# DLRM tower with a two-layer CIN: TensorE spreads the first chunk's layer-1 operands with zero-one matrices, and the order of gathers and products moves

## The chip, the cores and the metric

The kernel runs on one core of a Trainium2 chip. Its time is the device time of one execution in microseconds; the number for a kernel is the median of its runs. One further execution is recorded by the hardware profiler, and all rows below come from that one.

## The reference, cut to what matters

512 samples have 32 ids each. Each id picks a row of 32 floats from its table, so a sample becomes `e[32 fields, 32 dims]`. A compressed interaction network with two layers follows, then a small dense network.

```python
e = stack([tbl_f[ids[:, f]] for f in range(32)], axis=1)        # 512 x 32 x 32
prev = e
for W in (filter_0, filter_1):                                  # 1024 x 128, 4096 x 128
    z = einsum('bhd,bmd->bhmd', e, prev)                        # h: 32 fields, m: 32, then 128
    prev = relu(einsum('bpd,pn->bnd', z.reshape(b, h * m, d), W))
    outs.append(prev)
z = sum(concatenate(outs, axis=1), axis=-1)                     # 512 x 256
h = relu(concatenate([z, dense_ctx]) @ W_top1 + b_top1)
h = relu(h @ W_top2 + b_top2)
y = h @ W_top3
```

## The kernel before

**Chunks and tiles.** The 512 samples go through in 32 chunks (`CHUNKS`) of four tiles. A tile is four samples times 32 dims, 128 columns, one sample from each quarter of the batch; a chunk has 512 columns (`COLS`). Buffers are double, by the parity `p` of the chunk. The last chunks, and the first two, are written out; those between run in a hardware loop of two chunks an iteration (`over_chunks`).

**Layer 1.** Products of two fields of one sample are needed for all pairs. The kernel holds the fields on partitions four times (`x_same`: field f on partitions 4f to 4f+3) and a shifted copy (`x_shift`: for group g and shift s, field f + 4s + g). DVE multiplies the two into `z` (`products`, L482): `which` 0 is groups 0 and 1, 1 is groups 2 and 3, and 2 is the last shift of 16 fields from `x_pair` into `z_last`. PE multiplies `z` by the folded weights `v` into the bank `acc1` (`layer1`, L671): four fp32 matmuls and one of the last shift, whose operand is split into two rounded parts by ACT (`round_last`, L375) and POOL (`lower_last`, L256).

**How the operands get on the partitions.** POOL gathers the rows of a chunk by four indirect DMAs, one a tile (`gather`, L249), into `emb`. SP writes `emb` twice into the DRAM tensor `x_rows`, waits, and reads it back in the spread form with six DMAs (`chunk` of SP, L192): `x_same`, `x_shift` groups 0 and 1, `x_pair` three times, `x_shift` groups 2 and 3. SP starts on chunk c when layer 1 of chunk c - 2 is done and the four gathers of c have landed.

**Layer 2.** ACT (`relu1`, L362) and DVE (`lower`, L501) split layer 1's result into a high and a low part. For each tile PE makes eight banks of 512 (`layer2`, L690), three matmuls a bank. Even banks (`t_act`, a ring of two) are weighted by ACT (`weigh_tile`, L390), odd banks (`t_dve`, a ring of four) by DVE (`add_tile`, L520), which adds onto ACT's results in `prod`. POOL then folds `prod`: `halve` (L264) adds one half onto the other with an accumulating DMA, and `fold` (L279), called one tile later, adds the rest into `side`. `relu2` of ACT and `lower2` of DVE round the result, and PE sums it over the dims (`pooling`, L714) at the end of the next chunk. DVE's `lower2` of chunk c - 1 stands ahead of its tile 3 of chunk c.

**Order.** Each engine has its instructions in a fixed order, written by hand; semaphores tie the engines. In chunk c, DVE does: transpose of c+1 (the weights for layer 2), tile 0, products 0 of c+2, tile 1, products 2 of c+2, tile 2, `lower` and `pooling1` of c+1, `place`, `lower2` of c-1, tile 3, products 1 of c+2. PE does tile 0, layer 1 of c+1 (two matmuls), tile 1, layer 1 of c+1 (the rest), tiles 2 and 3, pooling. POOL, tile by tile: `halve` of the tile, gathers for chunk c+3, `fold` of the tile before. Behind `halve` of tile 0 it issues one gather, behind tile 1 one, behind tile 2 two.

**Start.** ACT loads layer 2's weights in eight pieces, six of them first and two once chunk 0's `x_rest` has landed; ACT rounds them (`upper_w`), DVE takes the remainder (`lower_w`). PE runs 14 dummy matmuls (`warm_up`) once `x_rows` of chunk 0 is written, then layer 1 of chunk 0 (`first_layer1`, L658), eight dummy matmuls, then the chunks. Products 0, 2 and 1 of chunk 1 stand before DVE's chunk 0. POOL gathers chunks 0 to 2, waits for ACT's rounding of chunk 1's last shift and does `lower_last(1, 1)` before its chunk 0.

Of the kernel before, what the change touches and what calls it, by code (L numbers as in the profile page):

```python
# [28 lines left out]
W_PIECES = BANKS  # L29
W_EARLY = 6  # L30
W_PIECE = FIELDS * MAPS // W_PIECES
# [7 lines left out]

def dlrm_tower(nc, table, ids, dense, w0a, w0b, w0c, w1, wt1, bt1, wt2, bt2, wt3, select, identity, out):  # L40
    fp32, f32r, i32 = mybir.dt.float32, mybir.dt.float32r, mybir.dt.int32
# [4 lines left out]
    with ExitStack() as ctx:  # L46
# [33 lines left out]
        cur2_hi = [sb(f"cur2_hi{p}", [128, TILES, MAPS], f32r) for p in range(2)]  # L80
        cur2_lo = [sb(f"cur2_lo{p}", [128, TILES, MAPS], f32r) for p in range(2)]
        sel_wide = sb("sel_wide", [128, SEL_WIDE])
        sel = [sb(f"sel{p}", [128, 128], f32r) for p in range(2)]
# [44 lines left out]
        x_rest = [sem(f"x_rest{p}") for p in range(2)]  # L128
        out_written = sem("out_written")
        ids_ready = sem("ids_ready")  # L130
        row_ids_ready = sem("row_ids_ready")
# [52 lines left out]
        def before(c, parity):  # L184

            return (c - parity) // 2

        @block.sync
        def _(sp):
            sp.dma_start(raw_ids[:, :], ids).then_inc(ids_loaded, 16)  # L190

            def chunk(c, p):  # L192
                turn = before(c, p) + 1

                wait(sp, layer1_done, c - 1)
# [8 lines left out]
                first, stride = src.offset, COLS  # L204

                def shifted(first_group, groups):

                    return bass.AP(src.tensor, first + first_group * stride,
                                   [[stride, FIELDS], [GROUPS * stride, SHIFTS], [1, groups * COLS]])

                sp.dma_start(x_same[p][:, :],
                             bass.AP(src.tensor, first, [[stride, FIELDS], [0, SHIFTS], [1, COLS]])).then_inc(x_first[p], 16)
                sp.dma_start(x_shift[p][:, 0:WHOLE, :].rearrange("p g c -> p (g c)"),
                             shifted(0, WHOLE)).then_inc(x_first[p], 16)
                for copy in range(3):
                    sp.dma_start(x_pair[p][copy * FIELDS:(copy + 1) * FIELDS, :, :],
                                 bass.AP(src.tensor, first, [[stride, FIELDS], [FIELDS // 2 * stride, 2], [1, COLS]])
                                 ).then_inc(x_rest[p], 16)
                sp.dma_start(x_shift[p][:, WHOLE:GROUPS, :].rearrange("p g c -> p (g c)"),
                             shifted(WHOLE, SPLIT)).then_inc(x_rest[p], 16)  # L220
# [20 lines left out]
        def _(pool):  # L241
            def stage(c, p):


                wait(pool, rows_written[p], before(c, p) * (16 * 2))
                wait(pool, weigh_ready, c - 1)
                nc.gpsimd.tensor_copy(row_ids[p][:, :], all_ids[:, bass.ds(c * TILES, TILES)]).then_inc(row_ids_ready, 1)

# [58 lines left out]


            pool.wait_ge(ids_ready, 1)
            for c in range(LEAD):  # L310
# [3 lines left out]
                gather(c % 2, range(TILES))  # L314
            lower_last(1, 1)

            def chunk(c, p):
                ahead = not (isinstance(c, int) and c + LEAD >= CHUNKS)
                first, final = isinstance(c, int) and c == 0, isinstance(c, int) and c == CHUNKS - 1
                for i in range(TILES - final):  # L320
                    if ahead and i == 0:
                        stage(c + LEAD, (p + LEAD) % 2)
                    here = final and i == TILES - 2
                    if not here:
                        halve(c, i, c + LEAD if ahead and i == 0 else None)
                    if ahead:
                        gather((p + LEAD) % 2, ((0,), (1,), (2, 3), ())[i])
                    if i > 0:
                        fold(c, i - 1, p)
                    elif not first:  # L330
                        fold(c - 1, TILES - 1, 1 - p)
                    if here:
                        fold(c, i, p, halve_here=True)
                    if not ahead and i % 2 == 1:

                        n = (c - (CHUNKS - LEAD)) * 2 + i // 2
                        if n < len(top_pieces):
                            lower_top(n)
# [6 lines left out]
        def _(act):  # L345
# [99 lines left out]
            for k in range(W_EARLY + 1, W_PIECES):  # L445
                upper_w(k)
            over_chunks(act, chunk, tail=TOP_PEEL)
# [21 lines left out]
        def _(dve):  # L469
# [12 lines left out]
            def products(c, p, which):  # L482

                turn = before(c, p) + 1
                if which == 0:
# [98 lines left out]

            transpose(0, 0)

# [6 lines left out]

            for k in range(W_EARLY):
                lower_w(k)
            for which in (0, 2, 1):
                products(0, 0, which)
            lower_w(W_EARLY)
            lower(0, 0)
            for k in range(W_EARLY + 1, W_PIECES):  # L600
                lower_w(k)
            pooling1(0, 0)
            for which in (0, 2, 1):
                products(1, 1, which)

            def chunk(c, p):
# [49 lines left out]
        @block.tensor  # L656
        def _(pe):
            def first_layer1():  # L658

                low = slice(0, FIELDS)  # L660
                for which, operands in enumerate(([(v[:, g, :], z[0][:, g, :]) for g in range(WHOLE)],
                                                  [(v_last[low, :], z_last[0][low, :])],
                                                  [(v[:, g, :], z[0][:, g, :]) for g in range(WHOLE, GROUPS)])):

                    pe.wait_ge(z_ready, which + 1)
                    for k, (weights, rows) in enumerate(operands):
                        last = nc.tensor.matmul(acc1[:, :], weights, rows, start=which == 0 and k == 0,
                                                stop=which == 2 and k == SPLIT - 1)
                last.then_inc(layer1_done, 1)
# [72 lines left out]
            warm_up(HOLD_UPS, t_dve[DRING - 1])  # L742

            def chunk(c, p):
                fixed = isinstance(c, int)
                more = not (fixed and c + 1 >= CHUNKS)
                layer2(c, 0, p)
# [7 lines left out]
                if not (fixed and c == 0):  # L755
                    pooling(c - 1, 1 - p)
# [116 lines left out]
```

## Time and profile before

| | |
|---|---|
| runs, median | 938.97 us (935.41 to 939.64, 3 runs) |
| the profiled execution | 945.5 us; its span, first to last instruction, 943.6 us |
| PE busy | 880.3 us, 93% of the span |
| PE weight loads | 660.3 us, 70% |
| DVE busy | 743.9 us, 79% |
| ACT busy | 655.2 us, 69% |
| POOL busy | 716.2 us, 76% |
| mean granted clock of TensorE | 0.993 of full speed |
| DMA | 131.16 MB, 139 GB/s over the span |

How to read the rows: in a timeline a row has its start in us from the start of the span, its duration in us, the engine, the line of the kernel, the operation, what it writes and reads, the shapes and how many instructions are merged; in square brackets stands how long the engine sat idle before it and what ended that. Durations of neighbouring instructions overlap, since engines are pipelined; the start of one to the start of the next is the pace. `SPq` and `ACTq` are DMA issues.

### The profile page before, as it was taken

The numbers are of one execution on the slowest core, as the hardware profiler recorded it, in microseconds if no ns is written. First come the engines' busy times: TensorE is split into PE (matmuls) and PEld (weight loads), VectorE is DVE, ScalarE is ACT, GpSimd is POOL, SyncE is SP. The second block draws the span as 40 slices with busy tenths as digits, with TensorE's granted clock in tenths as the row PEclk, the third lists the DMA queues.
The fourth block names the chain that finished last, engine by engine and source line by source line (L and its number), as shares of the span: only waits on it lengthen the run. The fifth ranks groups of instructions, "written<-read, shape, count | busy, mean of one in ns | idle before, by whom it ended". The sixth has DMA issues, their size and how long they took to land.

```text
span 943.6 us, 17792 instructions
## 1 busy us (share of the span) xinstructions
PE 880.3 (93%) x3519; PEld 660.3 (70%) x3519; DVE 743.9 (79%) x2328; ACT 655.2 (69%) x2199; POOL 716.2 (76%) x834
## 2 busy tenths in 40 slices
PE   2989979999999999999999999999999999999998
PEld 1567757777777777767777777777777767767774
DVE  2498857897777788777779877777987777898893
ACT  2567747777766777776677777677777767777772
POOL 5167869877888887787888778788877878787780
PEclk9999999999999999999999999999999999999998
DMA  6756666557676656766765676675567667555430
GB/s 178 209 114 154 152 142 143 117 136 160 147 159 156 134 117 141 162 146 155 161 130 114 147 164 146 152 164 128 116 147 163 147 147 161 124 123 146 90 67 1
DMA packets 55480, 131.16 MB, mean 139 GB/s; under 512 B 8100, under 2 KB 19332, under 8 KB 55461
## 3 DMA queue, kind: packets, MB, share of 16 engines
q0 software_dynamic: 22240, 68.17, 40.7%
q1 hardware_dynamic: 31538, 59.99, 20.2%
q10 hardware_dynamic: 1683, 2.80, 0.9%
q8 instruction: 6, 0.10, 0.0%
q14 instruction: 13, 0.11, 0.0%
HBM read 60.67 MB, written 4.20 MB: 69 GB/s over the span
## 4 chain that ended last, share of the span: by engine, by line
PE 35%; POOL 20%; DMA 18%; issue 18%; DVE 3%; SPq 2%; ACT 2%; POOLq 1%; DVEq 0%; ACTq 0%
DMA x_shift<-x_rows 10%; POOL prod L293 9%; POOL emb L252 6%; PE t_dve L710 5%; PE t_act L710 5%; PE t_act L712 5%; PE t_act L711 5%; PE t_dve L712 5%; PE t_dve L711 5%; DMA x_rows<-emb 5%; DMA emb<-table_dram,row_ids 4%; POOL prod L275 4%; PE acc L683 3%; ACT prod L402 2%; DVE prod L542 1%
## 5 line engine op out<-in xcount | busy, mean ns | idle before, releaser
L402 ACT ACTIVATE prod<-t_act,weigh 128x128 f32<-128x128 f32 x2048 | 580.5, 371 | 195.8 <-PE t_act L712 194.0
L542 DVE SCALAR_TENSOR_TENSOR prod<-t_dve,weigh,prod 128x128 f32<-128x128 f32 x1792 | 473.5, 335 | 1.1 <-DVE prod L542 0.5
L293 POOL TENSOR_TENSOR prod<-prod 128x512 f32<-128x512 f32 (+1 forms) x255 | 333.2, 1307 | 10.4
L710 PE MATMUL t_dve<-w_hi,cur_hi 128*128 128x512 f32 x512 | 204.0, 399 | 39.9 <-DVE prod L542 39.9
L494 DVE TENSOR_TENSOR z<-x_shift,x_same 128x1024 f32<-128x1024 f32 x64 | 100.3, 1568 | 162.6 <-DMA x_shift<-x_rows 162.6
L710 PE MATMUL t_act<-w_hi,cur_hi 128*128 128x512 f32 x512 | 216.4, 423 | 0.1
L712 PE MATMUL t_act<-w_hi,cur_lo 128*128 128x512 f32 x512 | 201.1, 393 | 0.0
L711 PE MATMUL t_act<-w_lo,cur_hi 128*128 128x512 f32 x512 | 200.5, 392 | 0.0
L712 PE MATMUL t_dve<-w_hi,cur_lo 128*128 128x512 f32 x512 | 200.4, 391 | 0.0
L711 PE MATMUL t_dve<-w_lo,cur_hi 128*128 128x512 f32 x512 | 200.2, 391 | 0.0
L252 POOL DMA_INDIRECT emb<-table_dram,row_ids x128 | 133.6, 1044 | 39.7 <-issue 38.9
L710 PEld LDWEIGHTS t_dve<-w_hi,cur_hi 128*128 128x128 f32 x512 | 96.5, 189 | 72.3 <-DVE prod L542 52.8
L274 POOL TENSOR_TENSOR tick<-v 128x4 f32<-128x4 f32 x126 | 38.2, 303 | 118.3 <-DVE prod L542 88.9
L710 PEld LDWEIGHTS t_act<-w_hi,cur_hi 128*128 128x128 f32 x512 | 96.6, 189 | 41.1 <-issue 15.3
L275 POOL DMA_DIRECT2D prod<-prod x126 | 114.7, 910 | 4.1 <-issue 2.0
L683 PE MATMUL acc<-z,v 128*128 128x512 f32 x248 | 116.4, 591 | 0.0
L711 PEld LDWEIGHTS t_act<-w_lo,cur_hi 128*128 128x128 f32 x512 | 96.7, 189 | 25.6 <-issue 7.4
L712 PEld LDWEIGHTS t_dve<-w_hi,cur_lo 128*128 128x128 f32 x512 | 96.6, 189 | 20.9
L712 PEld LDWEIGHTS t_act<-w_hi,cur_lo 128*128 128x128 f32 x512 | 96.4, 188 | 21.0
L711 PEld LDWEIGHTS t_dve<-w_lo,cur_hi 128*128 128x128 f32 x512 | 96.8, 189 | 19.8
L538 DVE SCALAR_TENSOR_TENSOR prod<-t_dve,weigh,prod 128x128 f32<-128x128 f32 x256 | 75.3, 332 | 4.7 <-ACT prod L402 4.7
L299 POOL TENSOR_TENSOR side<-prod 128x128 f32<-128x128 f32 x127 | 68.0, 536 | 10.0
(77 smaller groups left out, 456.1 us busy)
## 6 DMA issues: line engine op xcount, KB each, us to landing
prod<-prod POOLq DMA_DIRECT2D x126, 512.0 KB, 4.7
x_shift<-x_rows SPq DMA_DIRECT2D x64, 512.0 KB, 6.2
x_pair<-x_rows SPq DMA_DIRECT2D x96, 128.0 KB, 5.3
x_same<-x_rows SPq DMA_DIRECT2D x32, 256.0 KB, 5.2
x_rows<-emb SPq DMA_DIRECT2D x64, 64.0 KB
w_raw<-w_dram ACTq DMA_DIRECT2D x8, 256.0 KB, 4.2
emb<-table_dram,row_ids POOLq DMA_INDIRECT x128, 3.7
w_raw<-wt_dram SPq DMA_DIRECT2D x2, 512.0 KB, 5.4
```

Of the source, the lines that this page charges most:

```text
L252: nc.gpsimd.indirect_dma_start(emb[p][:, i * DIM:(i + 1) * DIM], None, table, bass.IndirectOffsetOnAxis(ap=row_ids[p][:, i:i + 1], axis=0) ...
L275: nc.gpsimd.dma_start(prod[i][:, dst, :].rearrange("x h n -> x (h n)"), prod[i][:, other, :].rearrange("x h n -> x (h n)"), accum_op=ALU.a ...
L293: nc.gpsimd.tensor_tensor(src[:, dst, :], src[:, dst, :], src[:, other, :], ALU.add).then_inc(folded, 1)
L299: nc.gpsimd.tensor_tensor(side[p][:, i, :], src[:, 0, :], src[:, 1, :], ALU.add).then_inc(side_ready, 1)
L402: last = nc.scalar.activation(prod[i][:, HEADS * k + j, :], t_act[k % ARING][:, j * MAPS:(j + 1) * MAPS], ACT.Copy, scale=weigh[p][:, i, h ...
L494: nc.vector.tensor_tensor(z[p][:, g, :], x_shift[p][:, g, :], x_same[p][:, None, :].to_broadcast([128, 2, COLS]), ALU.mult).then_inc(z_rea ...
L538: nc.vector.scalar_tensor_tensor(dst, src, w, dst, ALU.mult, ALU.add).then_inc(added, 1)
L542: nc.vector.scalar_tensor_tensor(dst, src, w, dst, ALU.mult, ALU.add).then_inc(added, 1)
L683: nc.tensor.matmul(acc1[:, :], v[:, g, :], z[p][:, g, :], start=g == 0, stop=False)
L710: nc.tensor.matmul(bank[:, :], cur_hi[p][:, cols], w_hi[:, w], start=True, stop=False)
L711: nc.tensor.matmul(bank[:, :], cur_hi[p][:, cols], w_lo[:, w], start=False, stop=False)
L712: nc.tensor.matmul(bank[:, :], cur_lo[p][:, cols], w_hi[:, w], start=False, stop=True).then_inc(done, 1)
```

## The change

- **Chunk 0 of layer 1.** A new input `spread` (128 x 5 x 128, zeros and ones) is loaded by SP. ACT and DVE copy each quarter of `emb[0]` to its own columns of a cleared tile `emb_apart` (`set_apart`). PE multiplies `emb_apart` by the five matrices (`spread_zero`), giving `x_same` in the bank `t_act[0]` and the four shifted groups in the four `t_dve` banks. ACT copies `x_same` to SBUF, DVE multiplies group by group from the banks (`products_zero`). SP loads only `x_pair` for the first 32 partitions for chunk 0.
- **Weights.** ACT issues all eight loads at the start. PE's dummy matmuls no longer wait for `x_rows`.
- **Chunk 0's order.** Products 0 of chunk 1 come between DVE's tiles 0 and 1 of chunk 0, products 2 and 1 behind tile 1; products 0 and 2 of chunk 2 behind tile 2; `lower` of chunk 1 behind tile 3. PE does layer 1 of chunk 1 behind tiles 1 and 2. `relu1(1)` stands behind ACT's tile 2. POOL's `lower_last(1, 1)` stands behind its `fold` of tile 1, in the turn of tile 2.
- **Every chunk.** POOL issues two gathers behind `halve` of tile 0 and two behind tile 1. DVE does products 0 and 2 of chunk c+2 together behind tile 1, and `place` behind tile 0.

```diff
+        def set_apart(copy, q):
+            rows = slice(q * FIELDS, (q + 1) * FIELDS)
+            copy(emb_apart[rows, q * RUN:(q + 1) * RUN], emb[0][rows, :]).then_inc(apart_ready, 1)
...
+            sp.dma_start(spread_sb[:, :, :], spread).then_inc(spread_loaded, 16)
...
+                if isinstance(c, int) and c == 0:
+                    sp.dma_start(x_pair[p][0:FIELDS, :, :], pair).then_inc(pair_zero, 16)
+                    return
...
+            nc.gpsimd.memset(emb_apart[:, :], 0.0).then_inc(cleared, 1)
...
-            lower_last(1, 1)
...
-                        gather((p + LEAD) % 2, ((0,), (1,), (2, 3), ())[i])
+                        gather((p + LEAD) % 2, ((0, 1), (2, 3), (), ())[i])
...
+                    if first and i == 2:
+                        lower_last(1, 1)
...
-                    if i == 0 and isinstance(c, int) and c == 0:
+                    if i == 1 and isinstance(c, int) and c == 0:
                         round_last(1, 1)
...
-                    if i == 1 and not (isinstance(c, int) and c + 1 >= CHUNKS):
+                    if i == (2 if isinstance(c, int) and c == 0 else 1) and not (isinstance(c, int) and c + 1 >= CHUNKS):
                         relu1(c + 1, 1 - p)
...
-            for k in range(W_EARLY):
-                load_w(k)
-            for k in range(W_EARLY):
-                upper_w(k)
-            act.wait_ge(x_rest[0], 16 * X_REST)
-            for k in range(W_EARLY, W_PIECES):
+            for k in range(W_PIECES):
                 load_w(k)
             act.dma_start(sel_wide[:, :], select).then_inc(sel_loaded, 16)
-            upper_w(W_EARLY)
+            for k in range(W_PIECES // 2):
+                upper_w(k)
+            act.wait_ge(gathered[0], 16 * TILES)
+            act.wait_ge(cleared, 1)
+            for q in (0, 1):
+                set_apart(nc.scalar.copy, q)
+            upper_w(W_PIECES // 2)
+            act.wait_ge(spread_done, 1)
+            nc.scalar.activation(x_same[0][:, :], t_act[0][:, :], ACT.Copy).then_inc(same_ready, 1)
+            for k in range(W_PIECES // 2 + 1, W_PIECES):
+                upper_w(k)
...
+            def products_zero():
+                dve.wait_ge(same_ready, 1)
+                for g in range(GROUPS):
+                    dve.wait_ge(spread_done, g + 2)
+                    last = nc.vector.tensor_tensor(z[0][:, g, :], t_dve[g][:, :], x_same[0][:, :], ALU.mult)
+                    if g % 2 == 1:
+                        last.then_inc(z_ready, 1)
+                dve.wait_ge(pair_zero, 16)
+                low = slice(0, FIELDS)
+                nc.vector.tensor_tensor(z_last[0][low, :], x_pair[0][low, 0, :], x_pair[0][low, 1, :],
+                                        ALU.mult).then_inc(z_ready, 1)
...
                 add_tile(c, 0, p)
-                if more2:
+                place(c, p)
+                if fixed and c == 0:
+                    products(1, 1, 0)
+                add_tile(c, 1, p)
+                if fixed and c == 0:
+                    products(1, 1, 2)
+                    products(1, 1, 1)
+                elif more2:
                     products(c + 2, p, 0)
-                add_tile(c, 1, p)
-                if more2:
                     products(c + 2, p, 2)
                 add_tile(c, 2, p)
-                if more1:
+                if fixed and c == 0:
+                    products(c + 2, p, 0)
+                    products(c + 2, p, 2)
+                elif more1:
                     lower(c + 1, 1 - p)
                     pooling1(c + 1, 1 - p)
-                place(c, p)
                 if not (fixed and c == 0):
                     lower2(c - 1, 1 - p)
                 add_tile(c, 3, p)
+                if fixed and c == 0:
+                    lower(c + 1, 1 - p)
+                    pooling1(c + 1, 1 - p)
...
+            def spread_zero():
+                pe.wait_ge(spread_loaded, 16)
+                pe.wait_ge(apart_ready, QUARTERS)
+                for k, bank in enumerate([t_act[0]] + t_dve):
+                    nc.tensor.matmul(bank[:, :], spread_sb[:, k, :], emb_apart[:, :], start=True,
+                                     stop=True).then_inc(spread_done, 1)
...
             pe.wait_ge(wh_ready, HEADS)
-            pe.wait_ge(rows_written[0], 16 * 2)
-            warm_up(WARM_UPS, t_dve[DRING - 1])
+            warm_up(WARM_UPS, t_act[1])
+            spread_zero()
...
                 layer2(c, 0, p)
-                if more:
+                if more and not first:
                     layer1(c + 1, 1 - p, range(0, 2))
                 layer2(c, 1, p)
                 if more:
+                    layer1(c + 1, 1 - p, range(0, 2) if first else range(2, GROUPS + 1))
+                layer2(c, 2, p)
+                if first:
                     layer1(c + 1, 1 - p, range(2, GROUPS + 1))
-                layer2(c, 2, p)
                 layer2(c, 3, p)
```

## Rows read from the trace of the kernel before

**Rows 1.** Waits of PE: line, waited for, us in total, times, longest.

```profile
PE t_dve L710 <- DVE prod L542: 39.9, 29, 5.4
```

**Rows 2.** Timeline of PE, two of the restarts after such a wait.

```profile
138.63 0.80 PE L710 MATMUL t_dve<-w_hi,cur_hi 128*128 128x512 f32 x1 [5.37 <-DVE prod L542]
...
193.80 0.51 PE L710 MATMUL t_dve<-w_hi,cur_hi 128*128 128x512 f32 x1 [1.13 <-DVE prod L542]
```

**Rows 3.** Timeline of PE, pooling at the ends of chunks 1, 3, 4 and 30.

```profile
89.94 0.39 PE L720 MATMUL acc_pool<-cur_hi,sel 128*128 128x512 f32 x1
...
150.53 0.39 PE L720 MATMUL acc_pool<-cur_hi,sel 128*128 128x512 f32 x1
...
176.73 0.39 PE L720 MATMUL acc_pool<-cur_hi,sel 128*128 128x512 f32 x1
...
893.53 0.39 PE L720 MATMUL acc_pool<-cur_hi,sel 128*128 128x512 f32 x1
```

**Rows 4.** Chain that ended last, 205 to 232 us: start us, us, what.

```profile
205.41 2.78 DMA emb<-table_dram,row_ids
...
212.15 6.24 DMA x_shift<-x_rows
...
221.37 0.51 PE t_dve L710
```

**Rows 5.** Timeline of DVE in the loop: products 0, and `place`.

```profile
245.85 2.02 DVE L494 TENSOR_TENSOR z<-x_shift,x_same 128x1024 f32<-128x1024 f32 x1 [4.93 <-DMA x_shift<-x_rows]
...
865.06 1.74 DVE L571 CAST sel<-sel_wide 128x128 fp32r x1
```

**Rows 6.** Windows: stretch, length, busy us (instructions) by engine, clock, DMA, GB/s.

```profile
124.80:152.40 27.60, 22.23 (x87) 16.89 (x86) 17.67 (x61) 15.97 (x55) 17.63 (x22) 0.94 0.65 144
152.40:180.00 27.60, 27.60 (x115) 21.12 (x114) 22.55 (x74) 21.11 (x74) 22.51 (x27) 1.00 0.66 145
```

**Rows 7.** Timeline of POOL in the loop, its one wait of a chunk.

```profile
196.93 0.58 POOL L274 TENSOR_TENSOR tick<-v 128x4 f32<-128x4 f32 x1 [3.11 <-DVE prod L542]
```

**Rows 8.** Timeline of ACT's queue and ACT at the start.

```profile
3.06 2.74 ACTq L354 DMA_DIRECT2D w_raw<-w_dram  x6
...
7.12 1.15 ACT L360 ACTIVATE w_hi<-w_raw 128x512 fp32r<-128x512 f32 x2
```

**Rows 9.** Timeline of PE up to 60 us.

```profile
15.11 5.12 PE L728 MATMUL t_dve<-w_hi 128*128 128x512 f32 x14 [15.11 <-DMA x_rows<-emb]
...
27.14 1.98 PE L667 MATMUL acc<-z,v 128*128 128x512 f32 x4
...
31.07 0.47 PE L710 MATMUL t_act<-w_hi,cur_hi 128*128 128x512 f32 x1
...
51.37 0.51 PE L710 MATMUL t_dve<-w_hi,cur_hi 128*128 128x512 f32 x1 [3.56 <-DVE prod L542]
```

**Rows 10.** Timeline of DVE up to 31 us.

```profile
11.25 0.31 DVE L480 STREAM_TRANSPOSE weigh<-emb 128x128 f32<-128x128 f32 x1 [4.74 <-DMA emb<-table_dram,row_ids]
...
22.03 1.22 DVE L494 TENSOR_TENSOR z<-x_shift,x_same 128x1024 f32<-128x1024 f32 x1 [6.79 <-DMA x_shift<-x_rows]
...
30.28 0.69 DVE L507 TENSOR_TENSOR cur_lo<-cur,cur_hi 128x512 fp32r<-128x512 f32 x1 [0.47 <-ACT cur L373]
```

**Rows 11.** Timeline of POOL in chunk 0.

```profile
38.43 1.51 POOL L261 TENSOR_TENSOR z_parts<-z_last,z_parts 32x512 fp32r<-32x512 f32 x1 [18.16 <-ACT z_parts L381]
...
43.80 0.97 POOL L275 DMA_DIRECT2D prod<-prod  x1 [0.30 <-issue]
45.07 1.07 POOL L252 DMA_INDIRECT emb<-table_dram,row_ids  x1 [0.30 <-issue]
...
57.64 2.18 POOL L293 TENSOR_TENSOR prod<-prod 128x512 f32<-128x512 f32 x2
59.90 0.79 POOL L299 TENSOR_TENSOR side<-prod 128x128 f32<-128x128 f32 x1
```

**Rows 12.** Page, part 6: issues, KB each, median us from issue to landing.

```profile
prod<-prod POOLq DMA_DIRECT2D x126, 512.0 KB, 4.7
```

More of the change, by code:

```diff
@@ L29 @@
 W_PIECES = BANKS
-W_EARLY = 6
 W_PIECE = FIELDS * MAPS // W_PIECES
@@ L37, with dlrm_tower @@
 LEAD = 3
-def dlrm_tower(nc, table, ids, dense, w0a, w0b, w0c, w1, wt1, bt1, wt2, bt2, wt3, select, identity, out):
+def dlrm_tower(nc, table, ids, dense, w0a, w0b, w0c, w1, wt1, bt1, wt2, bt2, wt3, select, identity, spread, out):
     fp32, f32r, i32 = mybir.dt.float32, mybir.dt.float32r, mybir.dt.int32
@@ L81, in dlrm_tower @@
         cur2_lo = [sb(f"cur2_lo{p}", [128, TILES, MAPS], f32r) for p in range(2)]
+        spread_sb = sb("spread_sb", [128, 1 + GROUPS, 128])
+        emb_apart = sb("emb_apart", [128, COLS])
         sel_wide = sb("sel_wide", [128, SEL_WIDE])
@@ L129, in dlrm_tower @@
         out_written = sem("out_written")
+        spread_loaded = sem("spread_loaded")
+        pair_zero = sem("pair_zero")
+        cleared, apart_ready = sem("cleared"), sem("apart_ready")
+        spread_done = sem("spread_done")
+        same_ready = sem("same_ready")
         ids_ready = sem("ids_ready")
@@ L204, in chunk @@
                 first, stride = src.offset, COLS
+                pair = bass.AP(src.tensor, first, [[stride, FIELDS], [FIELDS // 2 * stride, 2], [1, COLS]])
+                if isinstance(c, int) and c == 0:
+                    sp.dma_start(x_pair[p][0:FIELDS, :, :], pair).then_inc(pair_zero, 16)
+                    return
                 def shifted(first_group, groups):
@@ L215, in chunk @@
                 for copy in range(3):
-                    sp.dma_start(x_pair[p][copy * FIELDS:(copy + 1) * FIELDS, :, :],
-                                 bass.AP(src.tensor, first, [[stride, FIELDS], [FIELDS // 2 * stride, 2], [1, COLS]])
-                                 ).then_inc(x_rest[p], 16)
+                    sp.dma_start(x_pair[p][copy * FIELDS:(copy + 1) * FIELDS, :, :], pair).then_inc(x_rest[p], 16)
                 sp.dma_start(x_shift[p][:, WHOLE:GROUPS, :].rearrange("p g c -> p (g c)"),
@@ L246, in stage @@
                 wait(pool, weigh_ready, c - 1)
+                if isinstance(c, int) and c == 2:
+                    pool.wait_ge(apart_ready, QUARTERS)
                 nc.gpsimd.tensor_copy(row_ids[p][:, :], all_ids[:, bass.ds(c * TILES, TILES)]).then_inc(row_ids_ready, 1)
@@ L432, in chunk @@
                         round_last(c + 2, p)
-            for k in range(W_EARLY):
-                load_w(k)
-            for k in range(W_EARLY):
-                upper_w(k)
-            act.wait_ge(x_rest[0], 16 * X_REST)
-            for k in range(W_EARLY, W_PIECES):
+            for k in range(W_PIECES):
                 load_w(k)
             act.dma_start(sel_wide[:, :], select).then_inc(sel_loaded, 16)
-            upper_w(W_EARLY)
+            for k in range(W_PIECES // 2):
[9 more added lines that the diff above has]
+                upper_w(k)
             relu1(0, 0)
-            for k in range(W_EARLY + 1, W_PIECES):
-                upper_w(k)
             over_chunks(act, chunk, tail=TOP_PEEL)
@@ L482, in products @@
             def products(c, p, which):
-                turn = before(c, p) + 1
+                turn = before(c, p) + p
                 if which == 0:
@@ L583, in _ @@
                                     ALU.subtract).then_inc(v_ready, 1)
-            transpose(0, 0)
+            def products_zero():
[9 more added lines that the diff above has]
+                                        ALU.mult).then_inc(z_ready, 1)
             def lower_w(k):
@@ L592, in lower_w @@
                 nc.vector.tensor_tensor(w_lo[:, w], w_raw[:, w], w_hi[:, w].bitcast(fp32), ALU.subtract).then_inc(wl_ready, 1)
-            for k in range(W_EARLY):
+            for k in range(3):
                 lower_w(k)
-            for which in (0, 2, 1):
-                products(0, 0, which)
-            lower_w(W_EARLY)
+            dve.wait_ge(gathered[0], 16 * TILES)
+            dve.wait_ge(cleared, 1)
+            for q in (2, 3):
+                set_apart(nc.vector.tensor_copy, q)
+            transpose(0, 0)
+            lower_w(3)
+            products_zero()
+            for k in range(4, 6):
+                lower_w(k)
             lower(0, 0)
-            for k in range(W_EARLY + 1, W_PIECES):
+            for k in range(6, W_PIECES):
                 lower_w(k)
             pooling1(0, 0)
-            for which in (0, 2, 1):
-                products(1, 1, which)
             def chunk(c, p):
@@ L661, in first_layer1 @@
                 for which, operands in enumerate(([(v[:, g, :], z[0][:, g, :]) for g in range(WHOLE)],
-                                                  [(v_last[low, :], z_last[0][low, :])],
-                                                  [(v[:, g, :], z[0][:, g, :]) for g in range(WHOLE, GROUPS)])):
+                                                  [(v[:, g, :], z[0][:, g, :]) for g in range(WHOLE, GROUPS)],
+                                                  [(v_last[low, :], z_last[0][low, :])])):
                     pe.wait_ge(z_ready, which + 1)
@@ L667, in first_layer1 @@
                         last = nc.tensor.matmul(acc1[:, :], weights, rows, start=which == 0 and k == 0,
-                                                stop=which == 2 and k == SPLIT - 1)
+                                                stop=which == 2)
                 last.then_inc(layer1_done, 1)
@@ L735, in _ @@
             pe.wait_ge(wh_ready, HEADS)
-            pe.wait_ge(rows_written[0], 16 * 2)
-            warm_up(WARM_UPS, t_dve[DRING - 1])
+            warm_up(WARM_UPS, t_act[1])
+            spread_zero()
             pe.wait_ge(v_ready, 1 + 2)
             first_layer1()
-            warm_up(HOLD_UPS, t_dve[DRING - 1])
+            warm_up(HOLD_UPS, t_act[1])
             def chunk(c, p):
@@ L746, in chunk @@
                 more = not (fixed and c + 1 >= CHUNKS)
+                first = fixed and c == 0
                 layer2(c, 0, p)
-                if more:
+                if more and not first:
                     layer1(c + 1, 1 - p, range(0, 2))
@@ L751, in chunk @@
                 if more:
+                    layer1(c + 1, 1 - p, range(0, 2) if first else range(2, GROUPS + 1))
+                layer2(c, 2, p)
+                if first:
                     layer1(c + 1, 1 - p, range(2, GROUPS + 1))
-                layer2(c, 2, p)
                 layer2(c, 3, p)
-                if not (fixed and c == 0):
+                if not first:
                     pooling(c - 1, 1 - p)
@@ L842 @@
     turned[0] = 0.0
+    spread = np.zeros((QUARTERS, FIELDS, 1 + GROUPS, FIELDS, SHIFTS), np.float32)
+    to, by = np.arange(FIELDS)[:, None], np.arange(SHIFTS)[None, :]
+    spread[:, to, 0, to, by] = 1.0
+    for group in range(GROUPS):
+        spread[:, (to + by * GROUPS + group) % FIELDS, 1 + group, to, by] = 1.0
+    spread = spread.reshape(128, 1 + GROUPS, 128)
     arrays = {
@@ L860 @@
         "identity": np.eye(128, dtype=np.float32),
+        "spread": spread,
     }
```

## The prediction

> **What bounds the kernel now.** I read the page first: PE is busy 93% of the span, every other engine at most 79%. So an edit can win only where PE stands still, or ahead of its first useful matmul. The waits of PE come second. One entry makes up nearly all of it: PE waits for DVE to free a bank, 39.9 us in 29 waits [rows 1]. The timeline shows where: at the first odd bank of tile 2, once a chunk, typically 1.13 us, and once 5.37 us [rows 2]. The chain tells why. The last gather of a chunk takes 2.78 us to land, SP writes and reads back, the x_shift read takes 6.24 us, and 3 us after it PE restarts [rows 4]. DVE sits idle 4.93 us for that read just behind tile 0 [rows 5], the ring of four banks covers all but the last microsecond or so, and the rest is PE's wait. The circle closes: POOL issues that last gather behind tile 2, two tiles before DVE needs its data.
>
> What a chunk costs without the wait is in the trace too. From pooling to pooling, chunk 4 takes 176.73 - 150.53 = 26.20 us [rows 3], with PE busy through all of its window at full clock [rows 6]. The 29 chunks 2 to 30 take 893.53 - 89.94 = 803.59 us, 27.71 each [rows 3].
>
> **Steady chunks.** Two edits act on the circle. The last gather is issued behind tile 1 and not tile 2, about 5.5 us earlier (a tile is 24 matmuls at about 0.229 us, which is 26.20 us over the chunk's 99 rounded matmuls and four fp32 ones of 3.8 slots each, since two of those take 1.98 us with the tail of the last [rows 9]). And DVE needs the data behind tile 1 of the next chunk and not tile 0: one tile and two layer-1 matmuls later, 5.5 + 1.7 = 7.2 us. Together some 12 us of room, where 4.93 us of DVE idling were missing [rows 5]. The wait goes, and even the long one of 5.37 us fits in. Less room is left if the transfers wait for something new: SP's other condition for chunk c+3, layer 1 of c+1 done, holds behind tile 1 of chunk c, before the gathers have landed, so it adds nothing.
>
> What is late next? PE itself, if DVE, ACT and POOL hold 26.2 us.
> - DVE is busy 22.55 us in the window of chunk 4 [rows 6], 3.7 us free. Behind tile 1 it now has 2.02 + 0.7 us of products in a row [rows 5, 10]. A bank can be late by about 3.5 us (three bank pairs and half a one, 4.8 us, less the 1.05 + 0.2 us that DVE needs for the bank), so this is covered. `lower2` must end before PE's pooling; behind tile 2 DVE does about 2.1 us of work and PE a whole tile of 5.5 us. I cost it at nothing; without this cover each microsecond comes back 29 times.
> - ACT does nothing new in these chunks: nothing.
> - POOL has the same instructions; its one wait of a chunk is 3.11 us [rows 7], so its work is 27.71 - 3.11 = 24.6 us, 1.6 us below 26.2. Its first two turns grow to about 7.5 us, which tile 1 and layer 1 between them fill. The moved x loads (1664 KB from their sizes) now run beside the accumulating DMA of tile 2 instead of tile 3, and that DMA's fold comes some 6 us after its issue; it lands in 4.7 us in the median [rows 12]. Taken at nothing; bounds 0 and 2 us a chunk of waiting, of which 1.6 are covered, so up to 0.4 x 29 = 12 us.
>
> Sum: 803.59 - 29 x 26.20 = 43.8 us gained.
>
> At one place the Trainium skill speaks against this. SBUF — State Buffer, section "SBUF: two separate sides", says that DVE and GpSimd share a port pair under an exclusive lock, taken by a DVE operation with two SBUF inputs against a GpSimd one that reads SBUF. The trace agrees in kind: products 0 take 2.02 us in the loop against 1.22 at the start, when POOL was idle, and a copy took 1.74 us [rows 5, 10].
>
> **Start, PE's view.** Before, layer 1 of chunk 0 ends at 27.14 + 1.98 = 29.1 and layer 2 starts at 31.07 [rows 9].
> - ACT's queue: six weight loads take 2.74 us to issue, nine issues 4.1, so ACT is free at 3.06 + 4.1 = 7.2. 1.3 us for its table (5.8 to 7.12) and four pieces at 0.58 give 10.9 [rows 8].
> - PE: 14 dummies take 5.12 us [rows 9], now from about 11 to 16.3. `emb[0]` is complete at 11.25 [rows 10]; with 1 MB more in flight perhaps 1 to 2 us later. The copies (nearest row the transpose, 0.31 us) end by 14, hidden by the dummies. Without the dummies' cover a late gather counts in full.
> - Five spreading matmuls, fp32 like those of layer 1, a pair 1.98 us: about 0.88 each, end at 20.7. ACT's copy of the first bank hides behind them.
> - DVE's four products from PSUM: no row shows this form; nearest 0.69 us for 128 x 512, bounds 0.3 (nearly nothing, the transpose) and 1.22 (twice the columns) [rows 10]. At 0.69 they keep PE's pace and end at 21.5. At 1.22 they end 1.5 us later.
> - Layer 1: four matmuls 20.7 to 24.4, the last 25.2. That is 3.9 us sooner than before; layer 2 starts at 27.2. The moved `x_rows` write and read for chunk 0 are gone, so chunk 1's land before DVE asks (about 28 against 33).
>
> **Chunk 0, where it is given back.** Tile 0 to 32.7, tile 1 to 38.2, two layer-1 matmuls to 39.9, tile 2 to 45.4, two more to 47.1. The fifth matmul of layer 1 needs `lower_last(1, 1)`. Before, POOL did it ahead of its chunk 0, at 38.43 [rows 11]. Now `halve` of tile 2 stands ahead of it, which waits for all of tile 2. POOL: tile 0's halve 33.9 to 35.3, two gathers at 1.07 + 0.3 to 38; tile 1's halve at 39.4, gathers to 43.5, fold and side 2.2 to 3.2 + 0.8 to 47; tile 2's halve to 48.3, fold and side to 51.6, `lower_last` 1.5 to 53.1 [rows 11]. PE idles 6.0 us (bounds 4 and 8). Queued behind: PE's tile 3, and in ACT `relu1(1)` with the tile 3 behind it. After an idle of 5.37 us the clock was granted at 0.94 over 27.6 us, 1.6 us lost [rows 2, 6]; I add it. Tile 3 ends at 60.4. Then layer 2 of chunk 1 needs `lower(1)`, which DVE now does behind tile 3: 1.3 us for the last bank and 0.69 for it, a second new wait of 2.1 us. Chunk 1 starts at 62.5 and, at 25.7 us without a pooling in front, its pooling is at 88.2 against 89.94: gain 1.7. Before, this stretch also held an idle of 3.56 us that goes [rows 9]. So the start's gain is mostly spent inside chunk 0. The tail behind 893.53 is untouched.
>
> **Sum.** 43.8 + 1.7 = 45.5 us; span 943.6 to 898.1, profiled execution 945.5 to 900.0. The median of the runs, 938.97, is 6.5 us under the profiled execution. If they differ in what is not the kernel's waits, the median goes to 893.5. If the long wait (5.37 + 1.6 us) was of the profiled execution alone, the runs hadn't it to lose: 900.5. I take 897.
>
> **Rivals.**
> - The wait on `lower_last` in chunk 0 is short or absent. For it: POOL's folds with DVE waiting can be quick. Against: the wait for tile 2's last add can't be passed. It would give back up to 6.0 + 1.6: 889.
> - The chunks settle above 26.2. For it: POOL has only 1.6 us of room, and the fold of tile 2 may wait for its DMA under the x loads. Price 0.3 to 0.5 us a chunk, 9 to 14 us: 906 to 911.
> - Slower than before: POOL and DVE hold each other up. Now the two products stand together, `place` moves into POOL's busiest turn, and PE no longer gives slack. Six DVE operations a chunk can lengthen (three products, `lower`, `lower2`, `place`), the most seen being about 1.5 us: the copy took 1.74 us for 128 columns, where 512 take 0.69 [rows 5, 10]. DVE's room is 3.7 us to 26.2 and 5.2 to 27.71. From 5.2 us of lengthening a chunk on it is slower; six times 1.5 is 9, so 29 x 3.8 = 110 us at the worst, about 970 when half of the excess shows. Against: in the loop one of the six lengthened by 0.8 us, the others hardly, with POOL as busy. By the lock rule of the Trainium skill's page above, this is what would happen if the new order made every such pair meet.
> - The reordering does not touch the circle, and the start nets to zero: 938. That needs x_shift to be 12 us later than the sum says.
>
> **How the numbers follow.** Forecast 0.66, with its own range 890 to 903; the short wait in chunk 0 0.14; chunks above 26.2 0.14; slower by the ports 0.03; no effect 0.03. The range 886 to 911 takes in the second and most of the third. A change under 0.5%, 4.7 us, can't be told from none: faster 0.95, same 0.02, slower 0.03.
>
> **What would show it.** Right: PE's waits for DVE near zero in the loop, no idling of DVE for x_shift, pooling to pooling 26.2; PE's first layer-2 matmul near 27; an idle of about 6 us before the fifth layer-1 matmul of chunk 1 near 53, and about 2 us before chunk 1. Wrong: a wait once a chunk in a new place (PE for `cur_lo` at pooling, POOL for its DMA), products above 2 us, or a clock below full in chunks where PE never idles.

## The result, and the profile after

| | before | changed |
|---|---|---|
| runs, median | 938.49 us (4 runs) | 899.59 us (898.12 to 900.68, 4 runs) |
| ratio | | 0.959, 95% interval 0.956 to 0.962 |
| span of the profiled execution | 943.6 us | 897.2 us |
| PE busy | 93% | 97% |
| DVE busy | 79% | 86% |

Forecast 897 us, measured 899.6. PE's waits in the changed kernel, with the same columns as [rows 1] (the first line is the start of the kernel, before any weight is there):

```profile
PE t_act L782 <- ACT w_hi L379: 11.0, 1, 11.0
PE acc L741 <- POOL z_parts L278: 7.1, 1, 7.1
PE t_act L764 <- issue: 1.9, 1, 1.9
```

The 39.9 us of waits for DVE are gone as a whole. What is left lies in chunk 0, but for two waits of 0.5 us in the tail. The windows of the changed kernel, the second being the loop (columns as in [rows 6]):

```profile
0.00:90.50 90.50, 70.45 (x252) 50.20 (x253) 57.70 (x154) 47.52 (x148) 52.20 (x63) 0.94 0.62 157
...
200.00:800.00 600.00, 600.00 (x2456) 459.41 (x2455) 541.57 (x1654) 457.37 (x1562) 515.63 (x597) 1.00 0.66 153
```

PE is busy all of 600 us, at full clock. DVE is busy 541.57 of 600, or 23.6 us a chunk, where it was 22.55 [rows 6]. The pooling matmuls at the ends of chunks 1, 2 and 30 and the start of layer 2, which answer to [rows 3, 9], in PE's timeline:

```profile
27.28 0.47 PE L764 MATMUL t_act<-w_hi,cur_hi 128*128 128x512 f32 x1
...
54.51 0.80 PE L741 MATMUL acc<-z_parts,v_parts 96*128 96x512 f32 x1 [7.15 <-POOL z_parts L278]
55.11 0.63 PE L764 MATMUL t_act<-w_hi,cur_hi 128*128 128x512 f32 x1
...
64.81 0.47 PE L764 MATMUL t_act<-w_hi,cur_hi 128*128 128x512 f32 x1 [1.86 <-issue]
...
90.59 0.39 PE L774 MATMUL acc_pool<-cur_hi,sel 128*128 128x512 f32 x1
...
116.73 0.39 PE L774 MATMUL acc_pool<-cur_hi,sel 128*128 128x512 f32 x1
...
848.72 0.39 PE L774 MATMUL acc_pool<-cur_hi,sel 128*128 128x512 f32 x1
```

So the 46.4 us between the two spans fall into three parts. Start up to the first pooling: 89.94 before, 90.59 after, 0.65 lost. The 29 chunks: 803.59 before, 848.72 - 90.59 = 758.13 after, or 26.14 each, 45.5 gained. The tail: 943.6 - 893.53 = 50.1 before, 897.2 - 848.72 = 48.5 after, 1.6 gained without an edit there. DVE's group of products, which answers to [rows 5], before and after (busy us, mean ns of one, idle us ahead of it):

```profile
L494 DVE TENSOR_TENSOR z<-x_shift,x_same 128x1024 f32<-128x1024 f32 x64 | 100.3, 1568 | 162.6 <-DMA x_shift<-x_rows 162.6
...
L516 DVE TENSOR_TENSOR z<-x_shift,x_same 128x1024 f32<-128x1024 f32 x62 | 77.7, 1253 | 0.1
```

DVE's idling ahead of these products falls from 162.6 us to 0.1, in all chunks together.

### The profile page after: what moved, and what is told of

The parts are those of the page before. It is cut to its first block, busy times and chain, and to the rows that moved or that the text cites. A ratio compares the mean times of both kernels' runs of the same rounds, so it can differ in the third digit from the quotient of the medians.

```text
span 897.2 us, 17847 instructions
## 1 busy us (share of the span) xinstructions
PE 873.9 (97%) x3529; PEld 663.3 (74%) x3529; DVE 774.3 (86%) x2332; ACT 653.3 (73%) x2202; POOL 720.0 (80%) x835
## 4 chain that ended last, share of the span: by engine, by line
PE 92%; DVE 1%; ACT 0%; issue 0%; POOL 0%; DVEq 0%; ACTq 0%
PE t_act L764 13%; PE t_act L766 13%; PE t_act L765 13%; PE t_dve L764 13%; PE t_dve L766 13%; PE t_dve L765 13%; PE acc L737 11%; PE acc L741 1%; PE acc_pool L774 1%; PE acc_pool L776 1%; DVE prod L575 0%; PE t_act L849 0%; PE t_dve L842 0%; DVE prod L564 0%; PE t_dve L786 0%
## 5 line engine op out<-in xcount | busy, mean ns | idle before, releaser
L564 DVE SCALAR_TENSOR_TENSOR prod<-t_dve,weigh,prod 128x128 f32<-128x128 f32 x1792 | 482.3, 339 | 14.2 <-PE t_dve L766 9.3
L310 POOL TENSOR_TENSOR prod<-prod 128x512 f32<-128x512 f32 (+1 forms) x255 | 308.3, 1209 | 12.8 <-DMA prod<-prod 2.4
L764 PE MATMUL t_dve<-w_hi,cur_hi 128*128 128x512 f32 x512 | 200.2, 391 | 0.0
L269 POOL DMA_INDIRECT emb<-table_dram,row_ids x128 | 131.2, 1025 | 38.7 <-issue 37.6
L560 DVE SCALAR_TENSOR_TENSOR prod<-t_dve,weigh,prod 128x128 f32<-128x128 f32 x256 | 76.3, 338 | 76.0 <-ACT prod L421 76.0
L291 POOL TENSOR_TENSOR tick<-v 128x4 f32<-128x4 f32 x126 | 73.3, 582 | 80.1 <-DVE prod L564 45.7
L316 POOL TENSOR_TENSOR side<-prod 128x128 f32<-128x128 f32 x127 | 70.3, 553 | 10.0
L516 DVE TENSOR_TENSOR z<-x_shift,x_same 128x1024 f32<-128x1024 f32 x62 | 77.7, 1253 | 0.1
```

The lines of the kernel that those rows point to most:

```text
L269: nc.gpsimd.indirect_dma_start(emb[p][:, i * DIM:(i + 1) * DIM], None, table, bass.IndirectOffsetOnAxis(ap=row_ids[p][:, i:i + 1], axis=0) ...
L291: nc.gpsimd.tensor_tensor(tick[:, :], v[:, 0, 0:TILES], v[:, 1, 0:TILES], ALU.add).then_inc(ticked, 1)
L310: nc.gpsimd.tensor_tensor(src[:, dst, :], src[:, dst, :], src[:, other, :], ALU.add).then_inc(folded, 1)
L516: nc.vector.tensor_tensor(z[p][:, g, :], x_shift[p][:, g, :], x_same[p][:, None, :].to_broadcast([128, 2, COLS]), ALU.mult).then_inc(z_rea ...
L560: nc.vector.scalar_tensor_tensor(dst, src, w, dst, ALU.mult, ALU.add).then_inc(added, 1)
L564: nc.vector.scalar_tensor_tensor(dst, src, w, dst, ALU.mult, ALU.add).then_inc(added, 1)
```

## The experiments

They ran on three chips, each beside runs of the kernel before on its own chip. Ratios are to those. Where the intervals of two ratios overlap, the times alone don't tell the two versions apart, and the rows have to.

### The gathers alone

```diff
-                        gather((p + LEAD) % 2, ((0,), (1,), (2, 3), ())[i])
+                        gather((p + LEAD) % 2, ((0, 1), (2, 3), (), ())[i])
```

> The kernel before with the gathers alone moved (two behind tile 0, two behind tile 1), products where they were. Theory, either edit opens the circle by itself: the last gather is issued about 5.5 us earlier, DVE lacked 4.93 us behind tile 0 and PE about 1.4 us, so the wait of PE once a chunk goes and a chunk takes 26.1 to 26.3 us in place of 27.57; 29 chunks give about 40 us, some 895 to 902 us; DVE's idle for x_shift falls from 4.9 to under 1 us. Rival, the two edits are both needed (POOL's longer turns push the halving DMA and the gather back): the gain is under half, over 920 us.

Measured: 901.4 us, ratio 0.958 (0.955 to 0.962). PE's waits for DVE and two poolings:

```profile
PE t_dve L710 <- DVE prod L542: 2.1, 1, 2.1
```

```profile
87.14 0.39 PE L720 MATMUL acc_pool<-cur_hi,sel 128*128 128x512 f32 x1
...
847.01 0.39 PE L720 MATMUL acc_pool<-cur_hi,sel 128*128 128x512 f32 x1
```

(847.01 - 87.14) / 29 = 26.20 us a chunk. One wait is left of 29, in chunk 0, and DVE no longer idles for `x_shift` in the loop. This one edit opens the circle.

### DVE's order alone

```diff
                 add_tile(c, 0, p)
-                if more2:
-                    products(c + 2, p, 0)
+                place(c, p)
                 add_tile(c, 1, p)
                 if more2:
+                    products(c + 2, p, 0)
                     products(c + 2, p, 2)
```

> The kernel before with DVE's order alone changed (place behind tile 0, products 0 and 2 behind tile 1), gathers where they were. Theory: products 0 come 7.2 us later, more than the 4.93 us that DVE lacked, so PE's wait goes as well and a chunk takes 26.1 to 26.3 us: 890 to 900 us. In chunk 0 the wait for chunk 2's x_shift falls too, since DVE then holds tile 1 done and the ring of four banks covers tile 2. Rival: products 0 and 2 in a row delay tile 2's adds past the ring, and a wait of PE of about 1 us stays in tile 3: 920 to 935 us.

Measured: 895.3 us, ratio 0.951 (0.946 to 0.957); a chunk takes 26.16 us, from the poolings at 88.52 and 847.14. DVE's group:

```profile
L494 DVE TENSOR_TENSOR z<-x_shift,x_same 128x1024 f32<-128x1024 f32 x64 | 88.3, 1379 | 9.3 <-DMA x_shift<-x_rows 9.3
```

It too is enough by itself. The rival's wait in tile 3 shows in chunk 0 (3.88 us) and in the loop once, 0.32 us in chunk 4. For chunk 0 the expectation was wrong: DVE's waits for chunk 2's reads did not fall away, 2.04 us ahead of products 0 and 4.32 us ahead of products 2.

### Both loop edits, nothing of the start

The two diffs above together.

> The kernel before with both loop edits and nothing of the start (no spreading matmuls, chunk 0 as it was but for the two edits). Theory, the start edits give nothing and cost some microseconds in chunk 0: layer 2 starts at 31.1 us as before, but the idle of 3.56 us in chunk 0 and that of 7.15 us and 1.86 us of the changed kernel are all missing, so this is faster than the changed kernel by 5 to 8 us, 891 to 895 us. Rival, the start is worth its 3.8 us: 902 to 904 us.

Measured: 892.0 us, ratio 0.947 (0.944 to 0.950), whose interval lies under that of the changed kernel (0.956 to 0.962). A chunk takes (847.17 - 89.03) / 29 = 26.14 us. I had expected chunk 0 to be free of waits, and it isn't: PE waits 1.66 us for DVE in tile 1 and 3.69 us in tile 3. So 892.0 fell into the expected 891 to 895 partly by luck. Of the 7.6 us to the changed kernel's median, the rows show 1.6 up to the first pooling (89.03 against 90.59) and 1.6 in the tail; the profiled execution was the slowest of its four runs, at 895.9, and where the rest lies is open. PE's timeline, then DVE's:

```profile
56.87 0.77 PE L709 MATMUL t_dve<-w_hi,cur_hi 128*128 128x512 f32 x1 [3.69 <-DVE prod L542]
```

```profile
54.14 1.64 DVE L498 TENSOR_TENSOR z_last<-x_pair 96x512 f32<-96x512 f32 x1 [4.74 <-DMA x_shift<-x_rows]
```

In chunk 0 the last reads of chunk 2 are late, and DVE's tile 2 stands behind them. In SP's queue eight loads for the top network, issued from 30.76 to 34.5 us, stand directly ahead of chunk 2's write at 34.91, and its reads follow at 41.54. That these loads are the cause is read from the order; no run moved them.

### The start alone

The changed kernel with `gather` and, from chunk 1 on, DVE's order put back.

> The changed kernel with the gathers and DVE's order from chunk 1 on put back as before: the start edits alone. Theory: pooling of chunk 0 at 90 to 92 us against 89.9 before, a chunk 27.57 us as before, so 938 to 941 us, no gain. Rival, the start is worth its 3.8 us earlier first layer-2 matmul: 934 to 935 us.

Measured: 942.1 us (10 runs), ratio 1.0015 (0.999 to 1.004): no gain, and a little above the 938 to 941 expected. PE's waits, then its first two poolings:

```profile
PE t_dve L767 <- DVE prod L564: 28.9, 24, 2.0
...
PE acc L744 <- POOL z_parts L278: 8.4, 1, 8.4
```

```profile
93.68 0.39 PE L777 MATMUL acc_pool<-cur_hi,sel 128*128 128x512 f32 x1
...
120.03 0.39 PE L777 MATMUL acc_pool<-cur_hi,sel 128*128 128x512 f32 x1
```

The pooling at 93.68 is later than the 90 to 92 expected; POOL here has two more gathers ahead of `lower_last` in the turn of tile 2, and the wait is 8.4 in place of 7.1 us.

### Where the start's gain goes: lower_last earlier

Run beside the changed kernel itself, once more:

> The changed kernel unaltered, beside the two below on one chip. 897 to 901 us; pooling to pooling 26.1 us, idle of 7 us before the fifth layer-1 matmul of chunk 1, idle of 1.9 us before chunk 1.

Measured: 899.7 us, ratio 0.959 (0.956 to 0.961). Then with this edit:

```diff
                         gather((p + LEAD) % 2, ((0, 1), (2, 3), (), ())[i])
+                    if first and i == 1:
+                        lower_last(1, 1)
...
-                    if first and i == 2:
-                        lower_last(1, 1)
```

> The changed kernel with POOL's lower_last(1, 1) behind its gathers in the turn of tile 1, ahead of the halving of tile 2. Theory: that wait of PE (7.15 us, and about 2 us of half clock behind it) is the price of the order alone; POOL is done with it at about 47 us, as PE asks. 8 to 9 us faster than the changed kernel, 889 to 892 us; the idle of 1.9 us before chunk 1 stays. Rival: PE then waits at the same place for something else (chunk 2's x_shift under the top loads, as in the loop-only kernel), and under 4 us are won.

Measured: 894.9 us, ratio 0.952 (0.950 to 0.955), 4.8 us under the changed kernel, short of the 8 to 9 of the theory and a little over the rival's bound. The first pooling comes at 87.71, against 90.06 in the changed kernel profiled beside it, 2.4 us sooner. PE's timeline, then ACT's:

```profile
54.58 0.79 PE L764 MATMUL t_act<-w_hi,cur_hi 128*128 128x512 f32 x1 [4.07 <-ACT prod L421]
```

```profile
52.88 0.63 ACT L400 ACTIVATE z_parts<-z_last 96x512 fp32r<-96x512 f32 x1 [3.99 <-DVE z_last L520]
```

The wait on POOL is gone, and the next one stood behind it. ACT has the rounding of chunk 2's last shift between tiles 2 and 3, which waits for DVE's `z_last`, which waits for those late reads; PE waits for ACT to free a bank. The rival had the right transfer, on another engine than I had thought.

### lower(1) earlier as well

```diff
                 if fixed and c == 0:
                     products(c + 2, p, 0)
                     products(c + 2, p, 2)
-                elif more1:
+                if more1:
                     lower(c + 1, 1 - p)
                     pooling1(c + 1, 1 - p)
...
                 add_tile(c, 3, p)
-                if fixed and c == 0:
-                    lower(c + 1, 1 - p)
-                    pooling1(c + 1, 1 - p)
```

> As the one before, and lower(1) and pooling1(1) of chunk 0 ahead of DVE's tile 3. Theory: the second wait (1.9 us before chunk 1) goes too: 1.5 to 2 us under the one before, 887 to 890 us, and faster than the loop-only kernel by the 3.8 us that the start is worth. Rival: DVE waits there for ACT's relu1 and products of chunk 2, tile 3's adds come late and PE waits in tile 3 instead: no difference from the one before.

Measured: 889.9 us, ratio 0.948 (0.945 to 0.951). The 1.86 us ahead of chunk 1 are gone. The medians fall by 5.0 us, more than the 2 that this wait is worth; in the profiles the first pooling comes 4.0 us sooner, 1.0 of it before layer 2 starts and about 1 us in the clock behind the wait of 4.07, which is there in both. The gain of 3.8 us over the loop-only kernel is not shown: the ratios are the same (0.947, 0.944 to 0.950, there). In the profiles this kernel's first pooling comes 5.3 us sooner (83.73 against 89.03), but the two ran on different chips, and the difference stays open.

### Without the middle matmul of each bank

```diff
-                    nc.tensor.matmul(bank[:, :], cur_hi[p][:, cols], w_lo[:, w], start=False, stop=False)
```

> The changed kernel without the matmul of cur_hi by w_lo in each bank of layer 2, one of three (the output lacks that part). Theory: PE alone sets 26.14 us a chunk; 32 matmuls at 0.23 are 7.3 us less, 18.8, and then POOL with its 24.6 us of work a chunk is the bound: 24.3 to 25 us a chunk, 840 to 860 us. Rival, the chunk is bound by DVE and its order (22.6 us of work): 22.6 to 23.5 us a chunk, 795 to 820 us. If the time stays near 899 us, PE was not the bound.

Measured: 846.7 us, ratio 0.903 (0.900 to 0.906). Poolings at the ends of chunks 3 and 30 are at 134.34 and 796.03, so 24.51 us a chunk. The window of the loop, and DVE's products in it:

```profile
200.00:700.00 500.00, 434.72 (x1524) 271.55 (x1524) 500.00 (x1459) 386.02 (x1390) 456.40 (x527) 0.97 0.69 161
```

```profile
420.44 2.16 DVE L516 TENSOR_TENSOR z<-x_shift,x_same 128x1024 f32<-128x1024 f32 x1
422.52 1.22 DVE L520 TENSOR_TENSOR z_last<-x_pair 96x512 f32<-96x512 f32 x1
```

PE was the bound. The next is 24.5 us, the number that I had from POOL's work. Two engines are full at that length. DVE is busy all of the time. POOL is busy 91%, but in these 500 us it waits for other engines and for transfers only 2.4 us; the rest of its idle time is short gaps between its own instructions, 25.0 us of it ahead of its gathers. DVE's busy time was 22.55 us a chunk before. The two operations shown, 2.16 and 1.22 us, take 1.22 and 0.68 us at their shortest. So DVE's length goes with POOL's work beside it, and no run tells which of the two sets the 24.5 us.

### Chunk 2's last reads off the path

On top of the version with both early:

```diff
                 if fixed and c == 0:
                     products(c + 2, p, 0)
-                    products(c + 2, p, 2)
...
                 add_tile(c, 3, p)
+                if fixed and c == 0:
+                    products(c + 2, p, 2)
...
+                    if i == 0 and isinstance(c, int) and c == 1:
+                        round_last(2, 0)
-                    if i == 2 and not (isinstance(c, int) and c + 2 >= CHUNKS):
+                    if i == 2 and not (isinstance(c, int) and (c == 0 or c + 2 >= CHUNKS)):
                         round_last(c + 2, p)
```

> The kernel with both early, and in chunk 0 DVE's products 2 of chunk 2 behind tile 3 in place of tile 2, with ACT's rounding of them behind tile 0 of chunk 1. Theory: the idle of 4.07 us in tile 3 of chunk 0 is ACT standing behind that rounding, which waits for chunk 2's last reads (they land at 50 us); it goes, and about 4 us with it: 884 to 887 us. Rival: PE waits for another engine at the same place (DVE, for x_shift), or ACT's rounding delays chunk 1's tile 1 by as much: no difference from 889.9 us.

Measured: 886.5 us (6 runs), ratio 0.942 (0.938 to 0.946). All that PE waits for from 0 to the end:

```profile
PE t_act L782 <- ACT w_hi L379: 11.3, 1, 11.3
PE acc_pool L774 <- DVE cur_lo L587: 0.5, 1, 0.5
PE acc L876 <- ACT w_raw L488: 0.5, 1, 0.5
```

```profile
79.56 0.39 PE L774 MATMUL acc_pool<-cur_hi,sel 128*128 128x512 f32 x1
...
837.66 0.39 PE L774 MATMUL acc_pool<-cur_hi,sel 128*128 128x512 f32 x1
```

The first pooling is at 79.56, 11.0 us before the changed kernel's, and chunks take 26.14 us as there. This is the fastest version by its median; its interval overlaps that of the one before (0.945 to 0.951), and what sets them apart is the first pooling, 79.56 against 83.73, with the wait of 4.07 gone.

### The kernel before, a second time

> The kernel before, unaltered, profiled a second time. Theory: the one wait of 5.37 us in chunk 3 and the half clock behind it were of that one profiled execution; here every loop chunk waits about 1.1 us, the largest wait in the loop is under 2 us, and the span is 936 to 938 us. Rival: the long wait is the kernel's own and shows again at the same place, span near 943.

Measured: 942.1 us, span 940.2. PE's timeline:

```profile
54.51 0.79 PE L710 MATMUL t_dve<-w_hi,cur_hi 128*128 128x512 f32 x1 [6.42 <-DVE prod L542]
...
137.58 0.50 PE L710 MATMUL t_dve<-w_hi,cur_hi 128*128 128x512 f32 x1 [1.11 <-DVE prod L542]
```

In chunk 3, where [rows 2] have 5.37 us, the wait is 1.11. But chunk 0's wait is 6.42 us in place of 3.56 [rows 9], and the span is above the 936 to 938 expected. So neither long wait is fixed in size, and the other 11 runs of this kernel on this chip lie between 937 and 949 us.

## Why the prediction was right

**The circle.** Right, and shown from both sides: either edit alone removes the loop's wait, so the room of some 12 us was more than twice what was needed. 26.20 us a chunk was read from the one chunk that had no wait; measured 26.14.

**The start, PE's view.** Layer 2 starts at 27.28, as worked out (27.2), 3.8 us sooner than before. DVE's product from PSUM, for which no row stood, took 0.69 us:

```profile
20.02 0.69 DVE L611 TENSOR_TENSOR z<-t_dve,x_same 128x512 f32<-128x512 f32 x1 [0.17 <-PE t_dve L709]
```

**Chunk 0, where it is given back.** The mechanism was right, its size 2.4 us low. The wait on `lower_last` was 7.15 us, not 6.0: POOL's small `tick` took 1.65 us beside DVE's products, `side` took 1.31 us where I had 0.8, and the fold waited 1.13 us for the halving DMA, which I had taken as landed. POOL's timeline of the changed kernel:

```profile
39.74 1.65 POOL L291 TENSOR_TENSOR tick<-v 128x4 f32<-128x4 f32 x1 [0.69 <-issue]
...
50.66 2.05 POOL L310 TENSOR_TENSOR prod<-prod 128x512 f32<-128x512 f32 x2 [1.13 <-DMA prod<-prod]
...
53.21 1.25 POOL L278 TENSOR_TENSOR z_parts<-z_last,z_parts 32x512 fp32r<-32x512 f32 x1
```

Behind it eleven matmuls ran at a pace of 0.43 us in place of 0.23 (from 55.11 to 59.80; the granted clock from 50 to 60 us was 0.51, the level of 1.2 GHz), 2.2 us lost where I added 1.6. The first pooling came at 90.59, not 88.2: 0.65 us lost and not 1.7 won. The start alone points the same way, with its first pooling at 93.68 and a ratio of 1.0015.

**The sum.** 45.5 us were forecast between the spans, 46.4 measured, with errors that cancel in part: the start was 2.4 too good, the loop 1.7 and the tail 1.6 too low. The tail's code did not change; the granted clock in its last 26 to 28 us was 0.88 before and 0.93 after, and other kernels here show other values. Between the medians the gain is 38.9 us. I had set two cases beside each other, a gain of 45.5 (893.5 us) and one of 38.5 (900.5 us), the second if the long wait was of the one profiled execution. The second came out. The second profile of the kernel before agrees for the loop, where no wait is above 2 us, though it has a long wait of its own in chunk 0. The value of 897 between the two cases was a mean that no row gave, so that it lies only 2.6 us off is in part luck.

**DVE's room.** Here a bound was wrong without harm. I took 26.2 - 22.55 = 3.7 us as free, as if DVE's busy time were fixed. It isn't. From 200 to 800 us it comes to 22.5 us a chunk in the kernel before, 23.2 with DVE's order alone, 23.8 with the gathers alone and 23.6 in the changed kernel, for the same instructions. So DVE's work lengthened with the gathers alone, DVE's own order being as before. With PE's work cut it was 24.5, and the room left to DVE and POOL together was about 1.6 us, what I had given POOL. The rival of the ports needed 5.2 us of lengthening to be slower than before and got about 1, so it was not near. Its worst case doesn't follow from its own terms either: half of 110 us on top of 939 is 994, not 970. Of the operations that it named, `lower2`, `place` and the last shift's product lengthened in the mean between 200 and 800 us, from 0.68 to 1.47 us, 0.21 to 0.61 and 0.67 to 0.96, while the products of 128 x 1024 went down from 1.61 to 1.22.

The rule of SBUF — State Buffer, "SBUF: two separate sides", in the Trainium skill names the form of `lower2` (two SBUF inputs, beside POOL reading SBUF). The trace agrees in kind: a `lower2` of 2.34 us ran from 322.84 to 325.18, and POOL's fold of `prod` from 322.97 to 325.79. No run here took POOL's reads away, so the lock itself was not shown.

**What the start edits are worth.** The forecast saw that they give nothing, but not that they may cost. Loop edits alone: 892.0 us. With the start's edits: 899.6. With the start's edits and chunk 0's order mended: 886.5. The last is 0.942 (0.938 to 0.946) of the kernel before and the first 0.947 (0.944 to 0.950); the intervals touch, but in the profiled executions the first pooling is at 79.56 against 89.03. By the rows that is the two waits of 1.66 and 3.69 us, which the mended order lacks, with the lower clock behind the second, and layer 2 starting 2.0 us sooner (28.25 against 30.23 in that kernel's profile). No run has chunk 0's order mended without the spreading matmuls, so their own share was not measured.

## What to carry to other kernels

When one wait a chunk closes a circle through gather, DRAM and a product, measure the room that each cheap reordering gives, one at a time: here either of two was enough, and the costly edit of the start added nothing until three places in chunk 0's order behind it were put right. Before an instruction is moved in an engine's fixed order, list what it now stands behind and who needs it; `lower_last` behind a halving cost 7.15 us, and taking it away uncovered a wait of 4.07 us on ACT, so follow the chain until no wait is left. The free time of an engine, read as the chunk less its busy time, is an upper bound: DVE's instructions took from 22.5 to 24.5 us a chunk here, with other work beside them each time.

## What was not expected of the hardware

A POOL instruction on 128 x 4 elements, `tick`, took 0.20 us in about half of its places, about 1.1 us once or twice in a chunk of the loop, and 1.65 us at the most, beside DVE's products. DVE's product of 128 x 1024 took between 1.22 us and, behind chunk 0, 2.79 us. Its `lower2` took 0.68 us in every chunk of the loop before, and in the changed kernel 0.68 and 2.34 us nearly by turns from chunk to chunk:

```profile
401.48 0.68 DVE L585 SCALAR_TENSOR_TENSOR cur_lo<-side,cur_hi 128x512 fp32r<-128x512 f32 x1
...
427.43 2.34 DVE L585 SCALAR_TENSOR_TENSOR cur_lo<-side,cur_hi 128x512 fp32r<-128x512 f32 x1
```

PE ran 600 us without a gap with a granted clock of 1.00.
